# Two transformer layers on one core: the second half's layer norms between the layers in two parts, and the first context quarter of the second attention rounded on its own

## The reference, cut to what matters

```
x = x + attention0(layernorm(x), ctx)            # 16 batches of 56 tokens, ctx 1500 x 128
x = x + layernorm(x) @ factors.sum(0)/sqrt(8) + bias
h = layernorm(x)
q = rmsnorm(h @ Wq, gq)                          # 16 heads of 128
x = x + attention1(q, rmsnorm(ctx @ Wk, gk), ctx @ Wv)
x = x + moe(layernorm(x))                        # top 4 of 16 experts, and a shared one
```

## Time and profile before

| | us |
|---|---|
| median of 3 runs | 2154.72 (2154.16 to 2154.97) |
| the profiled execution, its device time | 2154.89 |
| its span in the profile | 2153.1 |
| PE busy | 2097.4 (97%) |
| DVE busy | 1639.5 (76%) |
| POOL busy | 1416.6 (66%) |
| ACT busy | 1079.0 (50%) |
| `between_layers`, PE's first to last matmul | 1203.68 to 1375.6 |

### The profile page before, as it was taken

The page is one execution under the profiler, slowest core; times in us unless marked ns, Lnnn a source line. Parts: engine busy times, 40 slices in busy tenths (PEclk is TensorE's granted clock), DMA queues, the critical chain, the costliest instruction groups (busy, mean ns, idle before and its releaser), DMA issues. The chain is left out here.

```text
span 2153.1 us, 27496 instructions
## 1 busy us (share of the span) xinstructions
PE 2097.4 (97%) x8514; PEld 1528.2 (71%) x8514; DVE 1639.5 (76%) x2584; ACT 1079.0 (50%) x3400; POOL 1416.6 (66%) x1061
## 2 busy tenths in 40 slices
PE   7999999999999999999999889999999999999999
PEld 7777677777777777777777468666666666665998
DVE  4889999999999999999997754556566665652577
ACT  3565555655565555555556227543434444432433
POOL 1477787778787887788776236287878778761221
PEclk9999999999999999999999999999999999999999
DMA  3000000000000000000000410011111110101110
GB/s 133 29 15 16 29 29 15 27 17 30 29 15 15 30 29 15 15 29 29 15 32 19 148 40 1 30 43 58 32 55 50 37 57 29 44 0 52 38 52 25
DMA packets 15140, 75.64 MB, mean 35 GB/s; under 512 B 1746, under 2 KB 2114, under 8 KB 13986
## 3 DMA queue, kind: packets, MB, share of 16 engines
q1 hardware_dynamic: 14994, 73.89, 10.5%
HBM read 72.97 MB, written 0.92 MB: 34 GB/s over the span
## 5 line engine op out<-in xcount | busy, mean ns | idle before, releaser
L539 ACT ACTIVATE l_prod_act<-l_prod_act 125x128 f32<-125x128 f32 x1152 | 342.0, 299 | 354.8 <-DVE l_prod_act L714 354.7
L634 POOL TENSOR_TENSOR l_prod<-l_prod 125x256 f32<-125x256 f32 x480 | 350.6, 738 | 239.6 <-DVE l_prod L714 239.4
L968 POOL TENSOR_TENSOR l_acc<-l_acc,l_probs 125x896 f32<-125x896 f32 x160 | 346.2, 2164 | 81.6 <-ACT l_probs L918 65.5
L714 DVE TENSOR_TENSOR l_prod<-l_side,xq 125x512 f32<-125x512 f32 x480 | 324.3, 676 | 45.2 <-PE l_side L823 38.6
L988 DVE TENSOR_TENSOR l_scaled<-l_slots,rk 125x896 f32<-125x896 f32 x192 | 206.9, 1084 | 197.7 <-PE l_slots L1053 197.6
L918 ACT ACTIVATE l_probs<-l_scaled 125x896 f32<-125x896 f32 x192 | 182.8, 952 | 320.7 <-DVE l_scaled L988 295.7
L628 POOL TENSOR_TENSOR l_acc<-l_acc,l_probs 125x896 f32<-125x896 f32 x160 | 339.5, 2122 | 0.0
L557 ACT ACTIVATE l_probs<-l_slots,mask_bias 125x448 f32<-125x448 f32 x384 | 224.7, 622 | 59.9 <-PE l_slots L775 54.1
L684 DVE SCALAR_TENSOR_TENSOR top<-l_side,mask_bias,top 125x448 f32<-125x448 f32 x330 | 216.3, 663 | 8.0 <-PE l_side L806 8.0
L539 ACT ACTIVATION_READ_ACCUMULATOR l_prod_act<-l_prod_act 125x1 f32 x1152 | 216.5, 188 | 0.0
L723 DVE TENSOR_REDUCE l_msq<-l_prod 125x4 f32<-125x256 f32 x480 | 195.8, 409 | 22.4 <-POOL l_prod L634 22.4
(11 more groups left out here) (257 smaller groups left out, 4635.1 us busy)
## 6 DMA issues: line engine op xcount, KB each, us to landing
land<-in_ctxT SPq DMA_DIRECT2D x32, 750.0 KB, 4.2
l_nat<-in_ctxN SPq DMA_DIRECT2D x16, 750.0 KB
post_we<-in_experts SPq DMA_DIRECT2D x20, 384.0 KB, 3.0
spare<-in_ctxN SPq DMA_DIRECT2D x8, 750.0 KB
nat<-in_ctxN SPq DMA_DIRECT2D x8, 750.0 KB
spare<-in_wo SPq DMA_DIRECT2D x2, 2048.0 KB, 8.8
spare<-in_wqT SPq DMA_DIRECT2D x4, 512.0 KB, 9.1
mid_fac<-in_factors SPq DMA_DIRECT2D x1, 2048.0 KB, 7.6
```

Of the source, the lines that this page charges most:

```text
L539: last = act.activation(whole, whole, ACT.Copy, accum_out=msq[:, t, 4 * g + c:4 * g + c + 1])
L634: pool.tensor_tensor(buf[:, :, 0:C // 2], buf[:, :, 0:C // 2], buf[:, :, C // 2:C], ALU.add).then_inc(s.half_sum, 1)
L714: dve.tensor_tensor(to[:, :, :], bank, xt.unsqueeze(1).to_broadcast([KT, 4, C]), ALU.mult).then_inc(s.side_dve, 1)
L968: pool.tensor_tensor(acc[:, :], acc[:, :], P[t % NP][:, :], ALU.add).then_inc(s.acc, 1)
```

## The change

1. `second_attention`: ACT rounds the first quarter (375 columns) of the first context, then the queries, then the other three quarters; POOL makes the low part of the first context in the same two pieces; PE's first scores wait for the first piece alone, tile 3 for the second. The semaphore counts behind it move up by one.
2. `between_layers`: the layer norm on DVE is cut into sums (statistics, aggregation, epsilon) and rows (reciprocal, normalised tiles). Half 0 does both at once, as before. Half 1 does the sums where the whole was, and the rows after the copy of `q 2` (first norm) and `q 9` (second norm).
3. ACT's roots of half 1 stand ahead of `q 2` and `q 9` rather than `q 3` and `q 8`.
4. `t1` and `f` of half 1 stand behind `q 6` rather than `q 5`, `t2` of half 1 behind `q 12` rather than `q 10`.
5. POOL's four added biases of half 1 follow `square_low` of heads 2 to 5 rather than 0 to 3.
6. DVE's `inverse_low(0)` stands ahead of the weights of `q 8` of half 1, rather than ahead of the first `r`.

```
-                need(sp, s.ctx_lo, b)
+                need(sp, s.ctx_lo, b + 1 if b > 0 else 0)
...
-            high_parts(0, 0)
+            first = S // 4
+            act.activation(chi[0][:, 0:first], land[:, 0:first], ACT.Copy).then_inc(s.ctx_hi, 1)
+            act.activation(qhi[0][:, :], m.qs[:, 0, :, :].rearrange("p h q -> p (h q)"), ACT.Copy).then_inc(s.q_hi, 1)
+            act.activation(chi[0][:, first:S], land[:, first:S], ACT.Copy).then_inc(s.ctx_hi, 1)
...
-            low_parts(0, 0)
+            for i, cols in enumerate((slice(0, S // 4), slice(S // 4, S))):
+                pool.wait_ge(s.ctx_hi, i + 1)
+                pool.tensor_tensor(clo[0][:, cols], land[:, cols], chi[0][:, cols].bitcast(F32), ALU.subtract).then_inc(s.ctx_lo, 1)
...
-                        pe.wait_ge(s.ctx_lo, b + 1)
+                        pe.wait_ge(s.ctx_lo, b + 2 if b > 0 else 1)
                         pe.wait_ge(s.q_lo, b + 1)
+                    if b == 0 and t == NT // 4:
+                        pe.wait_ge(s.ctx_lo, 2)
...
-    MID += [("t1", 1, 0), ("t1", 1, 1), ("f", 1, 0), ("f", 1, 1)] if h == 5 else []
-    MID += [("t2", 1, 0), ("t2", 1, 1)] if h == 10 else []
+    MID += [("t1", 1, 0), ("t1", 1, 1), ("f", 1, 0), ("f", 1, 1)] if h == 6 else []
+    MID += [("t2", 1, 0), ("t2", 1, 1)] if h == 12 else []
...
-def layer_norm_half_vector(dve, m, s, half):
+def layer_norm_half_sums(dve, m, s, half):
...
+def layer_norm_half_rows(dve, m, s, half):
...
-                if n < 4:
-                    add_bias(4 + n)
+                if 2 <= n < 6:
+                    add_bias(2 + n)
...
-                if job == ("t1", 0, 0) or job == ("q", 0, 3):
+                if job == ("t1", 0, 0) or job == ("q", 0, 2):
                     layer_norm_half_scalar(act, m, s1, half if kind == "t1" else 1)
-                if job == ("y", 1, 1) or job == ("q", 0, 8):
+                if job == ("y", 1, 1) or job == ("q", 0, 9):
                     layer_norm_half_scalar(act, m, s2, 0 if kind == "y" else 1)
...
+                if job == ("q", 1, 8):
+                    inverse_low(0)
                 if kind == "q" and i % 2 == 0 and H * half + i + NWQ - 1 < 2 * H:
                     weights_low(H * half + i + NWQ - 1)
...
                 if job == ("r", 0, 0):
-                    inverse_low(0)
                     dve.wait_ge(s.gain, 1)
...
-                        layer_norm_half_vector(dve, m, s1, half)
+                        layer_norm_half_sums(dve, m, s1, half)
+                        if half == 0:
+                            layer_norm_half_rows(dve, m, s1, 0)
...
                     dve.tensor_copy(qs_of(half, i), wide(bank)).then_inc(s.on_dve, 1)
+                    if i == 2:
+                        layer_norm_half_rows(dve, m, s1, 1)
+                    if i == 9:
+                        layer_norm_half_rows(dve, m, s2, 1)
```

More of the change, by code:

```diff
@@ L947, in _ @@
             batches(act, body)
-            act.wait_ge(s.ctx_lo, B)
+            act.wait_ge(s.ctx_lo, B + 1)
             for i in range(KC):
@@ L955, in low_parts @@
             def low_parts(b, par):
-                pool.wait_ge(s.ctx_hi, b + 1)
+                pool.wait_ge(s.ctx_hi, b + 2)
                 pool.tensor_tensor(clo[par][:, :], land[:, :], chi[par][:, :].bitcast(F32), ALU.subtract).then_inc(s.ctx_lo, 1)
@@ L1169, in layer_norm_half_vector @@
     dve.tensor_scalar(m.vareps[:, four], m.meanvar[:, four, 1], LN_EPS, None, ALU.add).then_inc(s.ln_var, 1)
+def layer_norm_half_rows(dve, m, s, half):
+    four = slice(4 * half, 4 * half + 4)
     dve.wait_ge(s.ln_std, half + 1)
@@ L1172, in layer_norm_half_vector @@
     dve.wait_ge(s.ln_rstd, half + 1)
-    for j in tiles:
+    for j in range(4 * half, 4 * half + 4):
         dve.tensor_scalar(m.xn[:, j, :], m.x[:, j, :], m.meanvar[:, j, 0:1], m.rstd[:, j:j + 1],
@@ L1391, in _ @@
                         dve.wait_ge(s1.xn, 4 * half + 4)
-                        layer_norm_half_vector(dve, m, s2, half)
+                        layer_norm_half_sums(dve, m, s2, half)
+                        if half == 0:
+                            layer_norm_half_rows(dve, m, s2, 0)
                 elif kind == "t2":
```

## The result

| | before | after |
|---|---|---|
| median, us, same chip | 2154.44 (2152.83 to 2154.97, 4 runs) | 2140.84 (2140.49 to 2141.8, 4 runs) |
| ratio | | 0.9939, 95% interval [0.9926, 0.9951] |
| profiled execution | 2154.89 | 2140.49 |
| its span | 2153.1 | 2138.7 |

A forecast was written before the change was run, and what follows sets the result against it. PE, busy 97% of the span, was taken as the bound, so only its stalls and slow-clock stretches could be won: 6.2 + 3.5 + 1.4 = 11.1 us off 2154.89, median forecast 2143.7, range 2142 to 2145.5 (2141.8 to 2148.0 with rivals).

The forecast's parts named there:

- Norms: `between_layers`, second half: splitting both norms and moving their users gains 6.2 us by `q 13`, 1.8 first norm, 4.4 second.
- low inverses: Ahead of the first `r`: made in DVE's idle time, PE's 2.07 us stall and 1.45 us slow stretch go; 3.5 us.
- second attention: Start of `second_attention`: low queries finish before PE's fifth fold ends, so first scores start there; 1.4 us, bounds 0 and 1.4.
- low weights of head 3: First norm, DVE: they wait for one POOL instruction, ready at 1268.5, so PE starts `q 3` at 1268.55 instead of 1270.76.
- three waits of 2.3 us together behind POOL's biases: First norm, PE: new waits of 1.45, 0.3 and 0.55 us for POOL's work, taken to cost no clock.
- Rival A: First norm: moved biases make POOL the bound, holding up heads 3 to 5, clock falls behind; 2146.3 us, chance 0.22.
- Rival B: Second norm: stall moves ahead of `q 13`, about 2 us plus 1.45 clock; low queries still meet POOL; 2148.6, chance 0.12.
- three signs of being wrong: `between_layers`: PE waits over 2 us for low weights, clock falls between 1273 and 1281, or a wait for `t2` rows.
- Rival C: Heads 3 to 15: strewn short waits keep the clock at 1.2 GHz; 4.0 us slower than before, 2158.7, chance 0.04.
- Another sign: `between_layers`, after the norms: the stretch from `q 13` to the first `r` keeps its length.
- The step that failed: Whole kernel: PE is busy 97% of the span, so outside the touched stages nothing can move by much.
- The base: Starting time of the sum: the profiled execution before the change, 2154.89 us, taken as 0.17 us above the median.

## Why the prediction was right, and where it was not

*The mechanism was right in each touched stage.* Norms 6.42 against 6.2 (first norm 2.3 against 1.8, second 4.1 against 4.4), low inverses 3.26 against 3.5, second attention 1.65 against 1.4; 11.33 against 11.1. Undoing each part alone gave its stage back: 6.4, 3.3 and 1.7. That the sum meets within 0.2 us is in part luck, since misses of +0.5, -0.3, -0.2 and +0.25 cancel.

*Norms, low weights of head 3.* Said: held by one POOL instruction, ready at 1268.5. By the Trainium skill, "SBUF — State Buffer", section "SBUF: two separate sides", a POOL instruction and a DVE instruction with two SBUF inputs (or in a two-port mode) share a port pair, and the one that starts first holds it for its whole length. The row of 0.41 us agrees: DVE got in before POOL's second low square, and that one was the longer for it. The low weights at 5.05 us do not follow from the rule alone, which gives the wait for one instruction: while they waited POOL ran the rest of one and five whole ones, none over 1.16 us, without a gap. So one DVE operation can lose several times running, and what decides it no run here shows. Said: three waits of 2.3 us together behind POOL's biases; found 1.78 (1.13, 0.39, 0.26).

*Rival A* (POOL the bound with a fall of the clock) didn't come: a wait of 1.13 us and two short ones within 4 us left the clock at 1.00. The prediction said that the trace doesn't show what a wait between 1.2 and 2.1 us does, and that is a misreading: PE's wait of 1.42 us for the low queries, at 1382.49, is in it, and the clock stayed up behind it:

```profile
1382.00:1385.50 3.50, 3.01 (x15) 2.78 (x16) 2.93 (x5) 1.40 (x2) 0.00 (x0) 1.00 0.73 248
1385.50:1389.00 3.50, 3.45 (x17) 2.75 (x16) 2.08 (x3) 1.99 (x3) 0.56 (x1) 1.00 0.32 133
```

It would have carried the choice to take nothing for the new wait of 1.45 us. But POOL's place in the order was the delicate part: the biases two heads earlier cost 4.07 us.

*Rival B*, the second stall moved, came in small: 0.67 us at `t2`, with the tiles at 3.46 us, over my upper bound of 3.0. A wait for the rows of `t2` was one of my three signs of being wrong, and it appeared; it goes with the 0.3 us by which the second norm gives less than said. *Rival C*, a low clock all along, didn't come.

*Low inverses.* Another sign, that `q 13` to the first `r` keeps its length, contradicts the prediction's own sum: the stall of 2.07 us lies ahead of that `r`, and the stage is 1.95 us shorter.

*Second attention.* 0.25 us more than said, because I took PE's idle time (1.42) for the gain. From start to start the first scores stood 2.45 us behind the fifth fold before (1382.49 - 1380.04) and stand 0.68 behind it now (1369.37 - 1368.69), 1.77 less: the idle time begins only where the last matmul ends, and in the rows matmuls that follow without a wait overlap. The first of them now takes 0.56 us instead of 0.44, which leaves 1.65.

*The step that failed* is the first sentence of the working: "outside the touched stages nothing can move by much", and with it the sum that ends behind the second attention and puts the last stage at nothing. I priced the low clock where PE's stalls went, 1.45 us a time, but not that shifting everything behind changes the moment at which later work comes, and with it the clock there. It gave 1.38 us. The trace of before had the row that tells it: a window behind the router with a clock of 0.60, behind a wait of 1.19 us, while one of 1.20 us between the layers had passed at 1.00. I had read the clock there and nowhere else. Whether it would be there after the change could not have been worked out from that one profile; that it might go or stay, 1.4 us, could have been, and as a bound of the range it would have held the time (2141.8 - 1.4 = 2140.4).

*The base.* 2154.89 was one execution. The seven groups of 4 to 17 runs of the kernel before have medians from 2153.6 to 2154.65, 2154.1 in the mean, where I started from 2154.72. That less 11.3 and 1.4 is 2141.4 against the 2140.84 measured. There is also a slip in the sum: 2154.89 - 11.1 - 0.17 is 2143.6, not 2143.7. Of the miss of 2.9 us, 1.4 is the router's stretch, 0.6 the base, 0.1 the slip and 0.2 the terms; about 0.5 stays open, which is no more than the groups of one kernel differ.

What is shown: the terms by undoing each part, and that the router's stretch hangs on the moment by the delays of 1.53 us in both kernels, which left every stage ahead of them as it was within 0.1 us. What is not: why just at those moments. By the Trainium skill, "TensorE: Matmul & The Clock Gate", section "Part 1: The HAM clock gate", the monitor behind the clock runs on its own and isn't restarted by a kernel; the alternation agrees with that, and so does the start: in the 17 profiles with the longer passage stretch the first `q` stands 1241.6 to 1241.9 us behind the beginning of the first low-clock stretch, wherever from 19.7 to 22.5 us that begins. The stretch itself is seen only in profiles: in both of before, in neither of after, and in one of the two of the version with the biases on DVE.

## What to carry to other kernels

Before costing a change that shifts everything behind it, list every stretch of low clock in the trace, also in stages that are not touched: those that no long wait explains can come or go with the shift, and each is a bound of the range (here 1.4 us of 13.6). Behind every wait of PE of 2.07 us and more between the layers the clock fell, in every profile; behind those of 1.6 us and less it didn't. Where a block on one engine holds up another, cutting the block, moving its users and moving the third engine's work were one edit here: leaving out one lost 45 to 94% of the gain. Measure with a ledger of stages from instruction to instruction, since one execution's start differs from another's by 2 us and more.

## What was not expected of the hardware

- A delay of 1.53 us on PE moves the granted clock of a stretch 60 us later from 1.00 to 0.52, or from 0.60 to 1.00, and added work can so cost next to nothing: 1.53 us more in the kernel before moved its last stage from 193.11 to 191.70, and the median by 0.5 us.
- Behind the router the low clock lasted 6.8 us rather than 3.4 in one profile (users one head later still), and the last stage took 194.82.
- One DVE operation of 0.41 us took 5.05 us beside POOL's back-to-back work, while five POOL instructions went by; another of the same form slipped in between at 0.41.
- One DVE addition over 1024 columns took 1.65 us, where POOL had needed four of 0.73 to 0.90, in the middle of its busiest stretch.
